# Second attention on one Trainium2 core: the value products of two key tiles in every second step instead of one tile in each step

## The reference, cut to what matters

```
def _L1_attn_ref(x, w_q, w_k, w_v, w_o):
    scale = 1.0 / sqrt(64)
    q = einsum('bsd,hdk->bhsk', x, w_q)      # 16 heads of 64
    k = einsum('bsd,hdk->bhsk', x, w_k)
    v = einsum('bsd,hdk->bhsk', x, w_v)
    scores = einsum('bhqk,bhmk->bhqm', q, k) * scale
    weights = softmax(scores, axis=-1)       # no mask: 512 x 512 for each head
    z = einsum('bhqm,bhmk->bhqk', weights, v)
    z = transpose(z, (0, 2, 1, 3)).reshape(b, s, h * dk)
    return x + einsum('bse,ed->bsd', z, w_o)
...
x = x + _L1_attn_ref(_layernorm(x), w_q, w_k, w_v, w_o)
```

## Time and profile before

| | us |
|---|---|
| median of 3 runs | 4505.9 |
| the profiled execution, its own time | 4506.45 |
| its span, first to last instruction | 4504.7 |
| first and last score matmul of the second attention begin at | 2648.1 and 3781.7 |
| last value product begins at | 3795.5 |
| PE busy, whole span | 4003.0 (89%) |

### The profile page before, as it was taken

One profiled execution on the slowest core, in us unless ns is written; L12 is line 12 of the kernel. 1 busy time (PEld: TensorE's weight loads), 2 busy tenths in 40 slices (PEclk: granted clock), 3 DMA queues, 4 the chain that ended last, 5 costly groups with the idle time before them and its releaser, 6 DMA issues. The chain is left out here.

```text
span 4504.7 us, 73929 instructions
## 1 busy us (share of the span) xinstructions
PE 4003.0 (89%) x26222; PEld 3087.4 (69%) x26222; DVE 2518.9 (56%) x4852; ACT 2003.3 (44%) x3837; POOL 956.5 (21%) x716
## 2 busy tenths in 40 slices
PE   4599959988974699879999969999999997899999
PEld 4499835555544599768888846666656664788888
DVE  4644346655645544356555546665666555565555
ACT  1566524444440666522333346555565554233332
POOL 0244312211200244313333300000000000133332
PEclk9999969999995799979999979999999999899999
DMA  3343210000003333210000010000000001000001
GB/s 116 94 102 78 35 53 15 15 21 16 25 26 102 117 82 80 33 52 15 10 11 14 24 61 1 11 10 11 1 11 10 11 6 41 20 11 10 14 10 38
DMA packets 144880, 159.27 MB, mean 35 GB/s; under 512 B 20320, under 2 KB 132704, under 8 KB 144352
## 3 DMA queue, kind: packets, MB, share of 16 engines
q1 hardware_dynamic: 117728, 113.15, 7.8%
q0 software_dynamic: 26880, 42.48, 5.0%
HBM read 105.01 MB, written 50.59 MB: 35 GB/s over the span
## 5 line engine op out<-in xcount | busy, mean ns | idle before, releaser
L1971 ACT ACTIVATE e_prob<-e_s_ps,e_small 128x512 f32<-128x512 f32 x512 | 346.7, 684 | 169.5 <-DVE e_small L2082 84.8
L2082 DVE TENSOR_REDUCE e_small<-e_s_ps 128x2 f32<-128x1024 f32 x256 | 313.2, 1223 | 168.3 <-PE e_s_ps L1848 164.3
L1388 ACT ACTIVATE b_pt<-b_t_ps 128x1024 f32<-128x1024 f32 (+3 forms) x256 | 180.8, 706 | 312.0 <-PE b_t_ps L1320 310.9
L903 POOL TENSOR_TENSOR f_h_lo<-f_hid,f_h_hi 128x512 fp32r<-128x512 f32 x144 | 188.2, 1307 | 518.2 <-ACT f_h_hi L874 518.2
L903 POOL TENSOR_TENSOR d_h_lo<-d_hid,d_h_hi 128x512 fp32r<-128x512 f32 x144 | 188.2, 1307 | 499.6 <-ACT d_h_hi L874 499.6
L2060 POOL TENSOR_TENSOR e_wide<-e_small,const 128x512 f32<-128x512 f32 x64 | 66.5, 1039 | 999.3 <-DVE e_small L2155 999.3
L1882 PE MATMUL e_z_ps<-e_pt,e_v 128*64 128x512 f32 x1024 | 275.5, 617 | 0.4 <-DVE e_zf L2162 0.4
L1861 PE MATMUL e_t_ps<-const,e_prob 128*128 128x128 f32 x2048 | 267.8, 274 | 6.1 <-ACT e_pt L1960 5.3
L1861 PEld LDWEIGHTS e_t_ps<-const,e_prob 128*128 128x128 f32 x2048 | 234.5, 141 | 51.1 <-issue 17.1
L1571 DVE TENSOR_REDUCE b_small<-b_s_ps 128x2 f32<-128x1024 f32 (+3 forms) x256 | 209.6, 819 | 84.7 <-PE b_s_ps L1299 80.7
L60 PE MATMUL d_h_ps<-d_x_hi,d_w_hi 128*128 128x512 f32 x576 | 231.0, 401 | 0.0
(11 more groups left out here) (544 smaller groups left out, 11832.4 us busy)
## 6 DMA issues: line engine op xcount, KB each, us to landing
ae_raw<-w_dram SPq DMA_DIRECT2D x16, 1024.0 KB
ce_raw<-w_dram SPq DMA_DIRECT2D x16, 1024.0 KB
d_raw<-m_dram SPq DMA_DIRECT2D x54, 128.0 KB, 2.3
f_raw<-m_dram SPq DMA_DIRECT2D x54, 128.0 KB, 2.3
b_xs<-x_dram SPq DMA_DIRECT2D x9, 512.0 KB, 3.9
ar_xs<-x_dram SPq DMA_DIRECT2D x8, 512.0 KB, 9.2
x_dram<-ar_xs SPq DMA_DIRECT2D x8, 512.0 KB, 7.7
rows_dram<-ar_xn POOLq DMA_DIRECT2D x8, 512.0 KB
```

What stands on the lines that cost most here:

```text
L903: gp.tensor_tensor(h_lo[:, g % 2], hid[:, g % 2], h_hi[:, g % 2].bitcast(F32), ALU.subtract).then_inc(hid_lo, 1)
L1388: act.activation(pt[:, kt % 2, a, :, 0:width], t_ps[:, :, 0:width], ACT.Exp).then_inc(p_ready, 1)
L1971: act.activation(prob[:, at], s_ps[:, at], ACT.Exp, bias=nmx[:, at:at + 1], accum_out=sums[:, buf, h * QT + s:h * QT + s + 1]).then_inc(p_ ...
L2082: dve.tensor_reduce(nmx[:, at:at + 2], s_ps[:, at:at + 2], AX.X, ALU.max, negate=True).then_inc(mx_ready, 1)
```

## The change

The value products are no longer issued one key tile in each step. Steps 0 and 2 issue none; step 1 issues those of the key tiles 0 and 1, and step 3 those of 2 and 3. What is computed and the order of the sums stay the same, and all other instructions keep their places.

```
-                        if has_prev:
-                            values(pair - 1, s, (pr - 1) % PAIRS, 1 - buf)
+                        if has_prev and s % 2:
+                            for kt in (s - 1, s):
+                                values(pair - 1, kt, (pr - 1) % PAIRS, 1 - buf)
```

## The result

The changed kernel takes 4579.3 us (median of 4 runs, 4572.9 to 4583.49) against 4504.87 us of the kernel before, now the median of four runs. The ratio is 1.0161, with a 95% interval of 1.0143 to 1.0178: +74.4 us, slower. The forecast was 4583 us, +76.3 on the profiled execution. The profiled execution of the changed kernel took 4572.9 us with a span of 4571.1.

A forecast was written before the change was run, and what follows sets the result against it. The prediction took PE, busy 99.67 of 100 us in the second attention, to bound the kernel. Waits for ACT's copy less saved form changes summed to +76.3 us on 4506.45, so 4583 us, range 4560 to 4601.

The forecast's parts named there:

- The sum: All terms in the second attention together: +76.3 us, between 55 and 95 from the bounds of the unknown prices.
- What bounds the stage: In the second attention PE is busy 99.67 of 100 us, so each microsecond it loses is the kernel's.
- Removed and added products: Steps 0 and 2 lose 1.01 us of value products each; steps 1 and 3 gain a second tile at 0.86.
- The gain of 0.15 a move: Each of 126 moves between steps, if nothing waits, saves 0.15 us on changes of form: 19 us at stake.
- The rival in which it decided alone: ACT's copy does not hold PE up and only fewer changes of form count: 4487 us, faster; chance 4%.
- The wait in step 1: PE waits 0.90 us before the spread sums for ACT's copy, +0.75 net in 56 ordinary steps: 42.0 us.
- The wait in step 3: PE waits for ACT's copy before the transposes: 24.0 + 7.7 + 3.7 - 2.1 + 0.3 us over the pairs.
- Step 1 of pair 2: The k projection waits 0.25 us for its bank until DVE's q_lo ends: +0.10 each, 7 times, 0.7 us.
- DVE at nothing: DVE's copy of the other bank ends before ACT's, so it adds no wait of PE: costed at nothing.
- Where batches meet: PE's dead time behind the value products between batches: taken at nothing, or 6 us less if a longer block hid it.
- The rival in which it falls: PE's longer waits lower the granted clock in the second attention: 14 to 28 us more, 4597 to 4611; chance 6%.
- the doubled blocks in step 1 buy nothing: PE comes 0.86 us later to the next step's transposes, which already had more than enough room: no gain.

The follow-up runs named there:

- e3: The changed kernel, with ACT's copy of head 0's transposes moved ahead of the step's two exponentials: 4483.7 us, against 4503.8 for the kernel before.
- e4: The kernel before, single key tiles kept, with only ACT's copy of head 0 moved ahead of the exponentials: 4500.1 us against 4503.8.
- e1: The kernel before with value products doubled in step 1 alone (none in step 0; steps 2 and 3 keep one tile each): 4550.8 us against 4503.8.
- e8: The changed kernel, with ACT's copy of head 0 placed between the two exponentials: 4505.3 us, against 4503.1 for the kernel before.
- e2: The kernel before with value products doubled in step 3 alone (none in step 2; steps 0 and 1 keep one tile each): 4539.8 us against 4503.8.
- e7: The changed kernel, with DVE's copy of head 1's transposes moved ahead of its job: 4580.6 us, against 4503.1 for the kernel before.
- e10: The kernel before with all four key tiles in step 1 and ACT's order as it was: 4582.1 us against 4503.1.
- e5: The kernel before with all four key tiles in step 3 and ACT's copy ahead of its exponentials: 4520.7 us against 4503.1.
- e6: The kernel before with all four key tiles in step 3 and ACT's order as it was: 4613.2 us against 4503.1.
- e9: The kernel before with all four key tiles in step 1 and ACT's copy ahead of its exponentials: 4475.3 us against 4503.1.

## Why the prediction was right

- *The sum.* +76.3 us forecast, +71.3 in the stage from pair 1 on, +74.4 between the medians. The mechanism is the one forecast, and the number lies in the range. That the whole time came within 4 us of 4583 is in part luck: about 3 us of it, as far as one profile of each kernel tells, come from other stages and from the lower clock at the head of this one. Of the 5 us between 76.3 and 71.3, some 4 are the handover below.
- *What bounds the stage.* PE did, at 99.67%; what it lost in the stage shows in the whole time.
- *Removed and added products.* The second tile was priced at 0.86 us from the tail, the block of two so at 1.87; it is 1.87. Transposes to scores cost what transposes to value products do: 0.97 against 0.96. The gain of 0.15 a move is borne out by e3 against e4, 14.2 us of 19 in the stage from pair 1 on and 16.4 by the medians. The rule of the Trainium skill that a change of the tiling mode drains the engine ("TensorEngine Tiling (Array Packing)", section Key Properties) agrees in direction with these 0.15 us. The rival in which it decided alone, 4487 us, did not come true, since the wait costs more than five times as much a move.
- *The wait in step 1.* Priced at +0.75 in 56 steps. The mechanism is shown by e1, e3 and e8. e1 gives +37.8 us from pair 1 on, where the prediction had 42.0 + 0.7. The size is a little less in most batches, since the handover from ACT's copy to the spread sums took 0.05 us (3043.71 to 3043.76) and not the 0.14 us that the earlier trace rows showed for the transposes: the term is some 0.09 us a step too large, about 4 us in all.
- *The wait in step 3.* Priced at 24.0 + 7.7 + 3.7 - 2.1 + 0.3 = 33.6 us; e2 gives +34.2 in the stage from pair 1 on. Pair 5's wait is 1.55 us, as 0.54 + 1.01 said.
- *Step 1 of pair 2.* Priced at +0.10 each, with a wait of 0.25 us of the k projection. The trace of the changed kernel shows it: the spread sums and the k projection start 0.59 us apart, against 0.41 before, so the wait is 0.18 us and the cost +0.03 by the same sum:

```profile
2990.18 0.66 PE L1869 MATMUL e_t_ps<-const,e_wide 128*128 128x128 f32 x4
2990.77 0.50 PE L60 MATMUL e_m_ps<-e_x_hi,e_wk_hi 128*128 128x512 f32 x1
```

- *DVE at nothing.* Right: e7 moved its copy and changed nothing. With ACT's copy out of the way in e3, DVE's held PE only in pair 5, three times, for 0.5 us in all.
- *Where batches meet*, taken at nothing: 1.4 us too little, since the idle time there grew from 2.6 us to 4.0, in five places and not seven (the turns of the loop; the first and the last batch are written out). That the value products at the end of a batch cover part of the turn only came out in e10.
- *The clock.* The rival in which it falls did not come true: waits of up to 1.6 us left it at 1.00. In e10, with 2.5 to 2.9 us idle, it fell behind four turns of five.
- *What the prediction did not see*, and did not need to, is the third handover, k_lo. It said that the doubled blocks in step 1 buy nothing, which is right for two tiles; that one of them covers the k_lo handover was missed, and e5 and e6 went wrong by it.

## What to carry to other kernels

Work that an in-order engine does between two uses of the same bank is cover: before moving it, subtract from its length the gap between the end of the other engine's release and the next use, place by place, and add up what turns into waiting. A stage at 99% busy can have just 0.1 us in hand. When such a move loses, look at what the *releasing* engine does ahead of the release: here one line moved on ACT, which by itself costs nothing (e4: 4500.1 against 4503.8), turned +74 us into -20 us. And ask of each place of a block what it hides there; the same block hid ACT's copy in steps 0 and 2, k_lo in step 1, and a part of the turn of the loop at the end of a batch.

## What the runs showed of the hardware

- The handover from an ended instruction on ACT or DVE to a waiting PE takes 0.14 to 0.15 us (0.14 in pair 5, 0.15 behind k_lo), but 0.05 us for the spread sums (3043.71 to 3043.76). It was 0.14 us for these too in the first and the last batch, whose instructions are written out, and 0.05 in the six batches of the loop; why is open.
- In the changed kernel the granted clock stayed at 1.00 through idle times of 0.3 to 1.6 us that came up to twice a pair. In e10 it fell to its lower level, 0.50, for 3.4 us behind idle times of 2.51, 2.56, 2.72 and 2.89 us, and did not behind one of 2.53. So the length of the idle time alone does not decide in this range.
- In this stage, at a clock of 1.00, a block of 128x64 products saves 0.15 us when it stands behind another of its form: 1.01 us for one, 1.87 for two, 3.59 for four in a row. The last is from this timeline of e9:

```profile
3042.07 3.65 PE L1882 MATMUL e_z_ps<-e_pt,e_v 128*64 128x512 f32 x16
3045.66 0.50 PE L1848 MATMUL e_s_ps<-e_k_hi,e_q_hi 64*128 64x512 f32 x2
```
